# Largest source value per destination: from the dense count matrix on VectorE instead of one-hots and matmuls per gathered group

## The reference, cut to what matters

```python
a_src = jnp.einsum('nhc,hc->nh', h, att_src)
a_dst = jnp.einsum('nhc,hc->nh', h, att_dst)
e = jax.nn.leaky_relu(a_src[src] + a_dst[dst], NEG_SLOPE)
m = jax.ops.segment_max(e, dst, num_segments=N)
e = jnp.exp(e - m[dst])
s = jax.ops.segment_sum(e, dst, num_segments=N)
alpha = e / (s[dst] + 1e-16)
out = jax.ops.segment_sum(h[src] * alpha[:, :, None], dst, num_segments=N)
```

## Time and profile before

| what | us |
|---|---|
| timed, median of 3 runs | 12570.55 |
| timed, lowest and highest | 12525.04, 12585.5 |
| profiled execution, span from first to last instruction | 17092.5 |
| in it, the max pass (9210 to 11846) | 2636 |
| in it, the pass of the sums (11850 to 13360) | 1510 |

### The profile page before, as it was taken

One profiled execution on the slowest core, in us unless ns is written; L12 is line 12 of the kernel. 1 busy time (PEld: TensorE's weight loads), 2 busy tenths in 40 slices (PEclk: granted clock), 3 DMA queues, 4 the chain that ended last, 5 costly groups with the idle time before them and its releaser, 6 DMA issues. The chain is left out here.

```text
span 17092.5 us, 246317 instructions
## 1 busy us (share of the span) xinstructions
PE 10085.8 (59%) x46104; PEld 7046.4 (41%) x46105; DVE 7941.5 (46%) x32217; ACT 4636.0 (27%) x14917; POOL 6838.7 (40%) x7337
## 2 busy tenths in 40 slices
PE   5555555541000266637894766667998556666659
PEld 4444444431000266633452222223777455555534
DVE  6333333330000388891105666566888555555540
ACT  0111111100000022200003666665444344444400
POOL 1444444457777400002002666664333355555500
PEclk8555555555555555557897888888999777777779
DMA  0000000000000366655683333334333222222337
GB/s 23 1 1 1 1 1 1 1 14 14 5 18 17 88 195 195 195 168 191 226 305 74 86 86 86 86 86 78 84 84 76 77 76 79 77 78 79 77 113 269
DMA packets 1388037, 1458.80 MB, mean 85 GB/s; under 512 B 259876, under 2 KB 1239808, under 8 KB 1349472
## 3 DMA queue, kind: packets, MB, share of 16 engines
q1 hardware_dynamic: 866640, 981.82, 18.4%
q0 software_dynamic: 234960, 339.86, 9.2%
q10 hardware_dynamic: 286272, 135.29, 2.7%
HBM read 1051.25 MB, written 404.95 MB: 85 GB/s over the span
## 5 line engine op out<-in xcount | busy, mean ns | idle before, releaser
L1427 POOL DMA_INDIRECT room<-tab_h,idx x1664 | 1581.4, 950 | 2336.1 <-POOLq L2466 1302.9
L1512 PE MATMUL banks<-acc,room 128*128 128x512 f32 x3328 | 1809.9, 688 | 866.4 <-DVE acc L1551 627.4
L855 POOL DMA_INDIRECT by_src<-big,h x1568 | 1515.0, 966 | 1877.2 <-DVE h L583 1428.0
L2172 POOL DMA_INDIRECT big<-tab_kv,idx x1664 | 1600.7, 962 | 1460.6 <-PE banks L2247 678.7
L1456 ACT ACTIVATE acc<-ident,room 128x128 f32<-128x128 f32 x5824 | 1768.0, 395 | 930.6 <-DMA x<-in_x 306.4
L855 POOL DMA_INDIRECT by_dst<-x,h x1456 | 1547.8, 1063 | 491.9 <-issue 462.0
L1151 DVE SCALAR_TENSOR_TENSOR acc<-acc,h,banks 128x128 f32<-128x128 f32 x3966 | 1084.4, 344 | 1377.4 <-remote 1108.5
L1512 PEld LDWEIGHTS banks<-acc,room 128*128 128x128 f32 x3328 | 667.2, 218 | 2008.3 <-issue 1298.7
L570 DVE SCALAR_TENSOR_TENSOR room<-banks,room 128x50 f32<-128x50 f32 x3136 | 437.0, 205 | 2077.4 <-remote 1047.5
L1042 PE MATMUL banks<-we2t,idx 128*128 128x8 f32 x3328 | 761.5, 358 | 966.3 <-ACT idx L1077 456.8
L1559 DVE TENSOR_REDUCE room<-banks 128x4 f32<-128x1024 f32 x832 | 1017.1, 1222 | 564.6 <-issue 272.3
(11 more groups left out here) (452 smaller groups left out, 19628.3 us busy)
## 6 DMA issues: line engine op xcount, KB each, us to landing
big<-cells SPq DMA_DIRECT2D x262, 1568.0 KB
cells<-acc SPq DMA_DIRECT2D x1985, 64.0 KB
cells<-acc ACTq DMA_DIRECT2D x1984, 64.0 KB
head_rows<-room SPq DMA_DIRECT2D x416, 264.0 KB
room<-head_rows SPq DMA_DIRECT2D x416, 264.0 KB, 2.9
acc<-w_rows SPq DMA_DIRECT2D x208, 512.0 KB
room<-cells SPq DMA_DIRECT2D x32, 1568.0 KB
room<-tab_h,idx POOLq DMA_INDIRECT x1664
```

The source lines that it names most:

```text
L855: pool.indirect_dma_start(self.target, bass.IndirectOffsetOnAxis(self.slots[:, t:t + 1], axis=0), self.rec[:, t, :], None).then_inc(self.s ...
L1427: pool.indirect_dma_start(far[:, m % BODY, 0:row], None, table, bass.IndirectOffsetOnAxis(k.idx[:, m:m + 1], axis=0)).then_inc(k.gathered[ ...
L1512: last = pe.matmul(k.psum[G * (j % MAX_RING) + t][:, :], oh, rhs, start=True, stop=True)
L2172: pool.indirect_dma_start(far[:, m % (G * RING), 0:2 * C], None, k.tab_kv_dram, bass.IndirectOffsetOnAxis(k.idx[:, m:m + 1], axis=0)).then ...
```

## The change

The gathers of POOL and the stores of SP stay: 1664 and 416. POOL no longer waits for the matmuls, only for the stores. The rest of the max pass goes. In its place a new `maximum_phase` reads the count matrix and works on it with DVE. For a strip of counts, the value `min(count, small)` is 0 where there is no edge and `small` where there is one, if `small` is below 1; DVE keeps the largest of these over all source blocks. `shift_phase` gets the values below 1: it also finds the largest value of each head, takes the power of two under the spread, doubles it, and divides by it.

The destination nodes are cut into 4 spans, of 13, 12, 12 and 12 blocks. For each span ACT loads 49 strips (one per source block, 128 partitions by 1664 or 1536 floats) into a ring of 8; DVE runs 4 instructions on each (one per head), with the head's running maximum as second input and output. At the end of a span PE transposes the maxima in pieces of 128 by 128, 4 to a bank, and DVE reduces each bank. None of the three uses a loop.

```diff
+SPANS = ((0, 13), (13, 12), (25, 12), (37, 12))
+SPAN = 13 * P
+STRIPS = 8
+def maximum_phase(nc, k):
...
+        @block.gpsimd
+        def _(pool):
+            for first in range(0, T, QUARTER):
+                if first >= BODY:
+                    pool.wait_ge(kept[first % BODY // QUARTER], first // BODY * 16)
+                    pool.sem_inc(k.passed, 1)
+                for m in range(first, first + QUARTER):
+                    pool.indirect_dma_start(
+                        k.gat[:, m % BODY, 0:A1], None, k.tab_h_dram,
+                        bass.IndirectOffsetOnAxis(k.idx[:, m:m + 1], axis=0)).then_inc(k.gathered[m % BODY], 16)
...
+        @block.scalar
+        def _(act):
+            for m, (c, src) in enumerate(steps):
+                lo, blocks = SPANS[c]
+                if m >= STRIPS:
+                    act.wait_ge(taken, (m - STRIPS + 1) * H1)
+                act.dma_start(strips[m % STRIPS][:, 0:blocks * P], cells[src, :, lo * P:(lo + blocks) * P])\
+                    .then_inc(loaded[m % STRIPS], 16)
...
+        @block.tensor
+        def _(pe):
+            for q, (c, h, b, width) in enumerate(quads):
+                if b == 0:
+                    pe.wait_ge(taken, ((c + 1) * NB - 1) * H1 + h + 1)
+                if q >= 8:
+                    pe.wait_ge(reduced, q - 7)
+                for u in range(width):
+                    ins = pe.transpose(k.psum[q % 8][:, u * P:(u + 1) * P], tops[h][:, (b + u) * P:(b + u + 1) * P],
+                                       k.ident[:, :])
+                ins.then_inc(turned, 1)
...
+        @block.vector
+        def _(dve):
+            for m, (c, src) in enumerate(steps):
+                lo, blocks = SPANS[c]
+                dve.wait_ge(loaded[m % STRIPS], 16 * (m // STRIPS + 1))
+                strip = strips[m % STRIPS][:, 0:blocks * P]
+                for h in range(H1):
+                    mine = tops[h][:, 0:blocks * P]
+                    if src == 0:
+                        ins = dve.tensor_scalar(mine, strip, k.small_asrc[:, src, h:h + 1], None, ALU.min)
+                    else:
+                        dve.wait_ge(taken, (m - 1) * H1 + h + 1)
+                        ins = dve.scalar_tensor_tensor(mine, strip, k.small_asrc[:, src, h:h + 1], mine,
+                                                       ALU.min, ALU.max)
+                    ins.then_inc(taken, 1)
+                if src == NB - 1:
+                    for q, (at, h, b, width) in enumerate(quads):
+                        if at == c:
+                            dve.wait_ge(turned, q + 1)
+                            dve.tensor_reduce(k.dense_max[:, lo + b:lo + b + width, h],
+                                              k.psum[q % 8][:, 0:width * P].rearrange("p (b s) -> p b s", s=P),
+                                              AX.X, ALU.max).then_inc(reduced, 1)
...
@@ shift_phase
     def src(dve, link, part):
-        link(dve, dve.tensor_reduce(part, k.asrc[:, :, :].rearrange("p b h -> p h b"), AX.X, ALU.min))
-        link(dve, dve.tensor_scalar(part, part, -1.0, None, ALU.mult))
+        by_head = k.asrc[:, :, :].rearrange("p b h -> p h b")
+        dve.tensor_reduce(part[:, H1:2 * H1], by_head, AX.X, ALU.max)
+        link(dve, dve.tensor_reduce(part[:, 0:H1], by_head, AX.X, ALU.min))
+        link(dve, dve.tensor_scalar(part[:, 0:H1], part[:, 0:H1], -1.0, None, ALU.mult))
...
+        link(dve, dve.tensor_tensor(spread, k.tmp[:, 0:H1], k.tmp[:, H1:2 * H1], ALU.add))
+        link(dve, dve.tensor_scalar(spread, spread, 1e-30, None, ALU.max))
+        link(dve, dve.tensor_scalar(bits.bitcast(I32), spread.bitcast(I32), 0x7F800000, None, ALU.bitwise_and))
+        link(dve, dve.tensor_scalar(above, bits, 2.0, None, ALU.mult))
+        link(dve, dve.reciprocal(under, above))
+        link(dve, dve.tensor_tensor(k.small_asrc, k.asrc[:, :, :], under.unsqueeze(1).to_broadcast([P, NB, H1]),
+                                    ALU.mult))
+        link(dve, copy(dve, k.top_scale, above))
...
-        run(pass_phase, "gat_max", "dst", k.tab_h_dram, A1, "max")
+        run(maximum_phase)
```

More of the change, by code:

```diff
@@ L196, in allocate @@
     k.chunk_room = room
+    k.small_asrc = k.wk[:, 0:NB * H1].rearrange("p (b h) -> p b h", h=H1)
+    k.dense_max = k.wk[:, 256:256 + NB * H1].rearrange("p (b h) -> p b h", h=H1)
+    k.top_scale = k.wk[:, 512:512 + H1]
     k.tmp = sb("tmp", [P, 256])
@@ L1260, in _ @@
             dve.memset(k.loc[:, T:T + G], PAD)
+SPANS = ((0, 13), (13, 12), (25, 12), (37, 12))
+SPAN = 13 * P
+STRIPS = 8
+def maximum_phase(nc, k):
+    n = "gat_max_"
+    loaded = [k.sem(f"{n}loaded{r}") for r in range(STRIPS)]
+    kept = [k.sem(f"{n}kept{q}") for q in range(QUARTERS)]
+    taken, turned, reduced, finished = (k.sem(n + s) for s in ("taken", "turned", "reduced", "finished"))
+    link = Link(k.sem(n + "step"))
+    base = k.gathered_base
+    k.gathered_base += 16 * IT
+    cells = k.cells_dram.rearrange("(s p d) c -> s p (d c)", p=P, d=NB)
+    strips = [k.big[:, r * SPAN:(r + 1) * SPAN] for r in range(STRIPS)]
+    tops = [k.acc[:, h * SPAN:(h + 1) * SPAN] for h in range(H1)]
+    quads = [(c, h, b, min(4, blocks - b)) for c, (_, blocks) in enumerate(SPANS) for h in range(H1)
+             for b in range(0, blocks, 4)]
+    steps = [(c, src) for c in range(len(SPANS)) for src in range(NB)]
+    with nc.Block() as block:
+        @block.gpsimd
[8 more added lines that the diff above has]
+                        bass.IndirectOffsetOnAxis(k.idx[:, m:m + 1], axis=0)).then_inc(k.gathered[m % BODY], 16)
+        @block.sync
+        def _(sp):
+            with sp.Fori(0, IT) as i:
+                for q in range(QUARTERS):
+                    for m in range(q * QUARTER, (q + 1) * QUARTER):
+                        sp.wait_ge(k.gathered[m], i * 16 + base + 16)
+                    columns = bass.ds((i * BODY + q * QUARTER) * A1, QUARTER * A1)
+                    sp.dma_start(k.head_rows_dram[:, columns].rearrange("p (m c) -> p m c", c=A1),
+                                 k.gat[:, q * QUARTER:(q + 1) * QUARTER, 0:A1]).then_inc(kept[q], 16)
+            for q in range(QUARTERS):
+                sp.wait_ge(kept[q], IT * 16)
+        @block.scalar
[39 more added lines that the diff above has]
+                                              AX.X, ALU.max).then_inc(reduced, 1)
+            dve.wait_ge(reduced, len(quads))
+            link(dve, dve.tensor_tensor(k.dense_max, k.dense_max, k.top_scale.unsqueeze(1).to_broadcast([P, NB, H1]),
+                                        ALU.mult))
+            dve.tensor_tensor(k.maxa[:, :].rearrange("p (b h) -> p b h", h=H1), k.dense_max, k.asrc[:, :, :], ALU.max)
@@ L1992, in use @@
         link(dve, dve.tensor_scalar(k.asrc[:, :, :], k.asrc[:, :, :], 0.0, None, ALU.max))
-    extreme_phase(nc, k, "low", src, H1, use)
+        spread, bits, above, under = (k.tmp[:, 8 + m * H1:8 + (m + 1) * H1] for m in range(4))
+        link(dve, dve.tensor_tensor(spread, k.tmp[:, 0:H1], k.tmp[:, H1:2 * H1], ALU.add))
[4 more added lines that the diff above has]
+        link(dve, dve.tensor_tensor(k.small_asrc, k.asrc[:, :, :], under.unsqueeze(1).to_broadcast([P, NB, H1]),
+                                    ALU.mult))
+        link(dve, copy(dve, k.top_scale, above))
+    extreme_phase(nc, k, "low", src, 2 * H1, use)
     with nc.Block() as block:
```

## The result

| kernel | timed, us (median, lowest to highest) |
|---|---|
| before | 12563.7 (12525.0 to 12585.5, 4 runs) |
| after | 12900.7 (12889.1 to 12925.8, 4 runs) |

The ratio is 1.0276, interval 1.025 to 1.0302: the change makes the kernel 2.8% slower. On another chip, beside its own runs of the kernel before, it was 1.0307 (1.0259 to 1.0355), 12951.8 against 12565.5. This time the profiled execution agrees with the timed ones (span 12924.0).

The account below looks back on a forecast made before the run. The max pass was taken as bound by POOL's gather issue, 2110 us. New stage 2080 + 376 + 10 = 2466, with 8 more 2474: 364 slower, 12935, less 35 gives 12900 us; range 12380 to 13130.

Parts of the forecast that it names:

- The hold: New max pass: while DVE works, POOL gets one gather per DVE instruction, 784 at 1.73 instead of 1.25, losing 376 us.
- The forecast sign: What a profile would show: held gathers longer than 0.95 us in the median, ending 0.8 us after a DVE instruction.
- The two-SBUF-input condition: A DVE instruction with two SBUF inputs holds back a POOL DMA near its start until that instruction ends.
- rival 1: New max pass: no hold, POOL stays at 1.25 us per gather; stage 2095 against 2110, time 12555; chance 0.17.
- The stage before: The old max pass lasts 2110 us in timed runs, bound by POOL's issue of gathers, not the profiled 2636.
- Its other such terms: Undisturbed rates elsewhere: ranking 1991 instead of 3370, second scatter and matrix 2278 instead of 4030, 8-head pass 2080 instead of 2930.
- Loads and stores: New max pass: ACT's 196 strip loads (157 MB) hidden and POOL's waits for quarter stores, both costed at 0.
- The 35 us taken off: Subtracted from 12935 for span ends, where DVE waits for PE and POOL goes free, and looseness in the 2110.
- the 2466 of the sum: New max pass: 2080 for gathers, 376 for the hold, 10 for first landing and last store.
- PE's clock: After the new stage PE starts from rest, costing 5 us at the next pass's start.
- the 4522 us: Profiled span's excess over the timed median, attributed to halts where POOL issues indirect DMAs; four stages' gains sum to 4507.
- rival 2: Old max pass: loop-edge halts, 104 times about 5 us, are real in timed runs; stage 2636 to 2474, time 12409; chance 0.15.

Follow-up runs that it names:

- the earlier trace: Also called the first trace: the profiled execution of the kernel before that the prediction read; its span was 17092.5 us, 4522 us longer than the timed median.
- the second trace: The kernel before, unchanged, profiled once more: 12576.6 us timed, span 12574.8.
- the version with 8 strips: The changed kernel with only the first 8 strips loaded, the other 188 loads left out, DVE's 784 instructions at full width: 12994.4 us, ratio 1.0308.
- the version with 10 blocks: The changed kernel with spans of 10, 10, 10, 10 and 9 blocks: ratio 0.9929 on the 17170 us chip, 12755.3 us and 1.0165 on another.

## Why the prediction was right

**The hold: right in kind and size.** Predicted was one gather per DVE instruction, 784 x 0.48 = 376 us. Measured: 588 intervals of 1.73 and 196 of 1.86 against 1.25 make 588 x 0.48 + 196 x 0.61 = 402 us, and POOL's busy time gives the same: 1664 x (1186 - 944) ns = 403. The 26 us over come from DVE's interval: the term took 1.83 us at 1664 columns and 1.70 at 1536, 1.73 in the mean, and the instructions start 1.86 and 1.73 us apart. The forecast sign holds as well: a held gather ends 0.82 us after a DVE instruction, where 0.80 was read from the earlier trace rows. The gathers in the last 1109 us are free, as said, and 866 where 880 were forecast.

The two-SBUF-input condition, read from one row of 2.80 us, is shown for that instruction by the pair of runs with the third operand in SBUF and in PSUM (1.0308 and 0.9992), and again at 896 columns (stages of 2815 and 2374 us). It was too narrow all the same. The gather at 3869.20 in the earlier trace rows, of which the prediction says only that the three-operand instruction didn't hold it, lasted 1.57 us instead of 0.95 and ended 0.83 us after an instruction with one SBUF input; the run with one input in SBUF shows 8 longer gathers beside the same kind.

The Trainium skill ("SBUF — State Buffer", section "Who interferes with whom") infers that making a DMA's descriptors is not stalled by such instructions; a gather is held by them all the same, 1.73 against 1.25 us, and rival 1 falls with it. Whether what is held is that making or the reading of the indices from SBUF, the runs don't tell.

**The stage before: right.** The prediction took 2110 us for the timed runs from the rates of undisturbed stretches; the second trace shows 2127. Its other such terms: the ranking 1991 against 1990; for the second scatter with the matrix a gain of 1752, and DVE's work on it ends 2158 us after the ranking where it took 3931 in the first trace, 1773 less; the 8-head pass, 2080, was 58 us too low (9604.4 to 11742.8).

**Loads and stores: costed at nothing, and nearly so.** With the loads POOL is busy for 1973.2 us, with 8 of them 1973.4. POOL's idle time for stores is 74.4 us in 152 waits, of which 46 are the usual 0.30: some 28 us that the sum did not have.

**The 35 us taken off: half wrong.** The stage before was 17 us longer than 2110, so that much of them is there. The new stage is 54 us longer than the 2466 of the sum, the 26 and the 28 above. From the first gather to the first instruction of the next stage (ACT and DVE start it together) the change takes 2520 us (5925.7 to 8445.2), before it is 2127: 393 slower, where the prediction had 364 and took 35 off. The rest of that trace is 44 us shorter than the other, 32 of them ahead of the stage, in code that is the same. On another chip the change cost 386 us (12951.8 - 12565.5), and the version with 8 strips, whose stage is the same, 397; beside them the 337 of the first comparison is low. So the 0.7 us between forecast and median is luck; the mechanism is worth some 390, about 60 more than the forecast's 329.

**PE's clock: 5 us, not seen.** It is granted 0.51 in the new stage and 0.97 in the pass of the sums, 0.96 there with the kernel before; the part from the next stage's start to the end is 12 us shorter with the change (4479 against 4491).

**The trace and the timed runs.** The prediction saw that the 4522 us don't belong to the timed runs. What they belong to it left open, and its words suggest the profiler. It is the chip, or its state: on one chip the timed runs themselves took 17170 us, on the others the profiled ones took 12575. So rival 2, real halts, is false for the chips of the verdict. On the other chip its condition holds, a stage of 2636 before; there the version with 10 blocks was a gain (0.9929) in spite of the 180 us. Little of that gain stands in the stage: from first to last gather it is 2567 us, against 2614 in the first trace, 47 of the 141 us. The rest would lie in code that is the same; no trace of the kernel before was taken on that chip. The change itself was not run there. An estimate: its 2507 us, with 868 gathers after DVE's work at 1.41 instead of 1.28, would be some 2620, against 2614 before. So rival 2's gain of 162 us is not to be expected even where its condition holds; that is not shown.

**What stays open.** Why a gather starves for 175 us with 1152 columns on one chip and never on the other. What differs in the traces is that POOL's waits without a releaser last up to 5.6 us there and at most 0.3 us on the other, where POOL has no wait longer than 0.35 us of any kind beside the 1152-column instructions; and that the starved gathers are 64 apart. That such a pause puts POOL out of step with DVE fits, but no run tested it, nor what happens every 64 gathers.

## What to carry to other kernels

Work moved to an idle engine is not free when its instructions hold up the engine that bounds the stage: ask what each new long DVE instruction with two SBUF inputs does to every indirect DMA beside it. If it must be, put one operand in PSUM (the hold went, 1.25 us a gather, though that version lost 174 us in a later pass), or choose the width so that one instruction lasts about as long as POOL's interval between DMAs (1024 columns here, 1.25 us; 1536 cost 400 us, and at 896 a gather passed only at every second instruction).

A trace with a span a third above the timed runs is of another condition: price each stage by its undisturbed stretches, and take a new profile before the rows of the slow one become terms of a sum.

## What the runs showed of the hardware that was not expected

- A gather of POOL and a DVE instruction with two SBUF inputs wait for each other. Which one pays depends on the lengths: from 1152 columns up POOL (1.33, 1.46, 1.73, 1.86 us), at 1024 DVE (1.25 in place of 1.20), at 896 POOL again and twice (2.12).
- A gather can be held for 63 to 180 us by a row of such instructions, until DVE does something else. It was seen on one chip of two: there in every span of 1152 columns and in one of 512, in none of 896 or 1280.
- A DVE instruction with one SBUF input that writes to SBUF (`tensor_scalar`, 1664 or 1536 columns f32) made gathers 1.55 to 1.78 us long; writing to PSUM it made none longer than 0.98.
- Two kinds of chip, or conditions of one: 12565 and 17170 us for the same kernel, with halts of about 6 us in loops beside indirect DMAs on the second. The Trainium skill ("Runtime: NRT & Kernel Launch", section "Instruction fetch mechanics") says that a branch to a target outside a small window costs a fetch by DMA, which is not every loop's edge, as the prediction read it. What the traces show is 6.45 us at the edge of PE's loop beside POOL's DMAs and 0.42 without them, and on a chip of the first kind halts in one loop of one kernel (3.50 us) and none in the same loop of another. What the halts are, the runs don't show.
- Loads with no pace (382 GB/s) slow POOL's gathers from 1.25 to 2.0 us by way of the stores that they wait for.
